# A transformer layer on 8 cores: value projections and expert-0 matmuls placed in three slots inside each layer-norm tile, and a loop exchange in the expert's first matmul

## The reference, cut to what matters

```python
def reference(x, w_in, b_in, w_out, b_out, router_w, w1, b1, w2, b2):
    xn = layernorm(x)                                   # per token, 1024 features
    # attention: att is summed over the key axis of its softmax only, so the
    # output of each head is v itself, times 1
    v = (xn @ w_in.T + b_in)[value part of each head]
    attn = v @ w_out.T + b_out
    # mixture of 8 experts, all of them computed, the best two weighted
    logits = xn @ router_w.T
    top2 values, indices -> softmax of the two -> weights
    h1 = gelu(einsum('bth,efh->btef', xn, w1) + b1)      # 4096 per expert
    y  = einsum('btef,ehf->bteh', h1, w2) + b2
    return x + attn + sum over the two experts of weight * y
```

## Time and profile before

| | us |
|---|---|
| median of 3 runs (4149.61 to 4161.2) | 4151.06 |
| the profiled execution's own time | 4155.26 |
| its span on the slowest core (core 3) | 4153.7 |
| spans of the 8 cores | 4136.3 to 4153.7 |
| mean granted TensorE clock, core 3 | 0.962 |
| PE busy | 3786.6 (91%) |

### The profile page before, as it was taken

One profiled execution on the slowest core, in us unless ns is written; L12 is line 12 of the kernel. 1 busy time (PEld: TensorE's weight loads), 2 busy tenths in 40 slices (PEclk: granted clock), 3 DMA queues, 4 the chain that ended last, 5 costly groups with the idle time before them and its releaser, 6 DMA issues.

```text
span 4153.7 us, 42034 instructions; the slowest of 8 cores (4136.3 to 4153.7 us)
## 1 busy us (share of the span) xinstructions
PE 3786.6 (91%) x17200; PEld 1688.6 (41%) x17200; DVE 372.6 (9%) x626; ACT 627.0 (15%) x610; POOL 667.0 (16%) x1073
## 2 busy tenths in 40 slices
PE   2466799999999999999999999999999999999994
PEld 1122244444444444444444444444444444444442
DVE  3331200000001010000001100000001010000001
ACT  0122102021120203020211202021110203020210
POOL 1001011111111111111111121111111111211110
PEclk9678899999999999999999999999999999999997
DMA  4324245555554555455556455555554555555554
GB/s 74 55 51 69 33 67 76 71 77 76 71 76 72 76 72 82 66 76 72 76 76 112 92 75 73 71 76 71 76 76 72 75 72 76 76 73 71 76 71 106
DMA packets 255706, 307.08 MB, mean 74 GB/s; under 512 B 51687, under 2 KB 182759, under 8 KB 255520
## 3 DMA queue, kind: packets, MB, share of 16 engines
q0 software_dynamic: 248608, 279.23, 48.2%
q1 hardware_dynamic: 6912, 25.17, 1.8%
HBM read 574.89 MB, written 8.39 MB: 140 GB/s over the span
## 4 chain that ended last, share of the span: by engine, by line
PE 88%; DVE 6%; DMA 3%; issue 2%; ACT 1%; DVEq 0%; SPq 0%; POOL 0%; ACTq 0%; POOLq 0%
PE P L339 43%; PE P L419 41%; DVE scr L433 3%; DMA wvw<-wvf 2%; PE P L188 1%; PE P L369 1%; DMA x_rot<-x 1%; PE P L247 1%; ACT vg L350 1%; DVE xnF L253 0%; DMA b1c_sb<-b1c 0%; DVE scr L239 0%; DVEq L46 0%; ACT L232 0%; DVE x_rot L463 0%
## 5 line engine op out<-in xcount | busy, mean ns | idle before, releaser
L419 PE MATMUL P<-wvw,vg 128*128 128x512 bf16 x8192 | 1815.6, 383 | 66.6 <-DVE scr L433 50.9
L339 PE MATMUL P<-xnF,wvw 128*128 128x512 bf16 x8192 | 1783.5, 381 | 6.6 <-DVE scr L433 6.6
L419 PEld LDWEIGHTS P<-wvw,vg 128*128 128x128 bf16 x8192 | 803.2, 99 | 1076.5 <-issue 146.2
L339 PEld LDWEIGHTS P<-xnF,wvw 128*128 128x128 bf16 x8192 | 803.0, 98 | 985.7 <-issue 30.5
L350 ACT ACTIVATE vg<-P,b1c_sb 128x1024 bf16<-128x1024 f32 x512 | 570.7, 1115 | 2850.0 <-PE P L339 2849.9
L396 POOL DMA_DIRECT2D wvw<-w2r x512 | 360.1, 706 | 1586.1 <-PE P L419 1512.0
L322 POOL DMA_DIRECT2D wvw<-w1r x512 | 271.3, 533 | 1555.6 <-PE P L339 1555.6
L433 DVE SCALAR_TENSOR_TENSOR scr<-P,wmap_sb,scr 128x512 f32<-128x512 f32 x256 | 192.1, 750 | 3251.6 <-PE P L419 3227.5
L188 PE MATMUL P<-xnF,wvw 128*128 128x512 bf16 x256 | 88.1, 513 | 46.8 <-DMA wvw<-wvf 46.8
L247 PE MATMUL P<-scr 128*128 128x128 f32 x128 | 26.6, 377 | 99.2 <-DVE scr L239 80.9
L178 POOL DMA_DIRECT2D wvw<-wvf x32 | 28.2, 886 | 276.2 <-PE P L188 276.1
(11 more groups left out here) (40 smaller groups left out, 194.8 us busy)
## 6 DMA issues: line engine op xcount, KB each, us to landing
wvw<-w1r POOLq DMA_DIRECT2D x512, 256.0 KB, 4.3
wvw<-w2r POOLq DMA_DIRECT2D x512, 256.0 KB, 4.4
x_rot<-x SPq DMA_DIRECT2D x32, 512.0 KB, 4.6
wvw<-wvf POOLq DMA_DIRECT2D x32, 256.0 KB, 5.3
out<-x_rot SPq DMA_DIRECT2D x16, 512.0 KB, 3.4
wo_sb<-wo POOLq DMA_DIRECT2D x8, 256.0 KB, 10.8
b1c_sb<-b1c POOLq DMA_DIRECT2D x1, 128.0 KB, 13.8
scr<-iden POOLq DMA_DIRECT2D x1, 64.0 KB, 5.6
```

The costliest lines, as they stand in the source:

```text
L339: pair=pair: t.matmul(pair[:, j * 512:(j + 1) * 512], w1sl[:, sl * 1024 + fc * 128: sl * 1024 + fc * 128 + 128], xnF[:, fc * T + half * 10 ...
L419: t.matmul(W2B[tl], vg[:, f1c * 1024 + tl * 128: f1c * 1024 + (tl + 1) * 128], w2sl[:, sl * 1024 + (f1c % 2) * 512: sl * 1024 + (f1c % 2) ...
```

## The change

There are two parts. The body of `emit_vp_unit` is the body of the loop over `vc` in `emit_vproj`, word for word, and is left out of the diff below.

1. `emit_vproj` is split into `emit_vp_unit(ts, vc)`, one unit each with the same body. `emit_A` calls a function `pump()` at three places: behind the emission of L239 (so on PE ahead of the transposes L247), behind L253 (on PE ahead of the logits) and behind L290 (on PE ahead of the transpose of the weights). Each `pump()` takes the first entry of a list `fills` and emits it, or does nothing where the list is empty. The 8 units of a block enter the list after every fourth tile; the 16 first-matmul groups of expert 0 enter it after tile 7, behind the units of block 1. What is left after tile 15 is emitted in a row.
2. In `emit_h1_group` the two inner loops are exchanged: all 8 matmuls of the first 512 tokens, then the 8 of the second, in place of both for each weight block. This holds for all 512 calls of the inner body, 8192 matmuls.

```diff
-    def emit_vproj(ts):
-        for vc in range(NFC):
...
+    def emit_vp_unit(ts, vc):
...
-    def emit_A(tt):
+    def emit_A(tt, pump):
@@ behind tensor_scalar L239
+        pump()
         p.wait("tensor", "dcst", n_cst)
         p.wait("tensor", "dve", tok_xnt[tt])
@@ end of emit_A
-        if DO_B and tt % 4 == 3:
-            emit_vproj(tt // 4)
@@ emit_h1_group
-            for fc in range(NFC):
-                for j in range(2):
+            for j in range(2):
+                for fc in range(NFC):
                     tok = p.do("tensor",
...
@@ main part
-    for tt in range(8):
-        emit_A(tt)
-    for tt in range(8, NTT):
-        if DO_C:
-            emit_h1_group(0, 0, 2 * (tt - 8))
-            emit_h1_group(0, 0, 2 * (tt - 8) + 1)
-        emit_A(tt)
+    fills = []
+    def pump():
+        if fills:
+            fills.pop(0)()
+    for tt in range(NTT):
+        emit_A(tt, pump)
+        if DO_B and tt % 4 == 3:
+            ts = tt // 4
+            fills += [(lambda ts=ts, vc=vc: emit_vp_unit(ts, vc))
+                      for vc in range(NFC)]
+        if DO_C and tt == 7:
+            fills += [(lambda g=g: emit_h1_group(0, 0, g))
+                      for g in range(NF1C // 2)]
+    while fills:
+        fills.pop(0)()
```

More of the change, by code:

```diff
@@ new lines, in emit_vp_unit @@
+    def emit_vp_unit(ts, vc):
+        idx = 8 * ts + vc
+        pair = SP[idx % 2]
+        sl = vc % 2
+        prev = (ts, vc - 2) if vc >= 2 else ((ts - 1, 6 + vc) if ts >= 1 else None)
+        if prev is not None:
+            p.wait("gpsimd", "pe", tok_vpmm[prev])
+        nqv[sl] += 1
+        p.do("gpsimd", lambda g, vc=vc, sl=sl: g.dma_start(
+            wvf_sl[:, sl * 1024:(sl + 1) * 1024].rearrange(
+                "p (c n) -> p c n", c=NFC),
+            d_wvf[vc].rearrange("c p n -> p c n")), inc=DQ[sl], inc_by=16)
+        wait_pair(idx % 2)
+        p.wait("tensor", DQ[sl], 16 * nqv[sl])
+        p.wait("tensor", "dve", tok_xnFev[4 * ts + 3])
+        vps = pair[:, 0:512]
+        for fc in range(NFC):
+            tok = p.do("tensor", lambda t, fc=fc, sl=sl, ts=ts, vps=vps:
+                       t.matmul(
+                vps,
+                wvf_sl[:, sl * 1024 + fc * 128: sl * 1024 + (fc + 1) * 128],
+                xnF[:, fc * T + ts * 512: fc * T + (ts + 1) * 512],
+                start=(fc == 0), stop=(fc == NFC - 1)),
+                inc=("pe" if fc == NFC - 1 else None))
+        tok_vpmm[(ts, vc)] = tok
+        p.wait("scalar", "pe", tok)
+        tok_vev[idx] = p.do("scalar", lambda s, vc=vc, ts=ts, vps=vps:
+                            s.activation(
+            optF[:, vc * T + ts * 512: vc * T + (ts + 1) * 512],
+            vps, AF.Identity, bias=bvc_sb[:, vc:vc + 1]), inc="act")
+        set_pair(idx % 2, "act", tok_vev[idx])
```

## The result

Over ten runs of each, the ratio of the changed kernel to the kernel before is 0.9747, 95% interval [0.9728, 0.9765]: 4054.6 us (median) against 4154.9. The forecast was 4050, a ratio of 0.976 to the 4151.1 known then.

A forecast was written before the change was run, and what follows sets the result against it. Bound before the output projection: each tile's DVE/ACT/PE chain, taking turns with groups. That stretch falls from 413.7 to 122.0 + 122.0 + 69 = 313 us, a gain of 100.7 against the median 4151.1: 4050, range 4026 to 4082.

The forecast's parts named there:

- What bounds the first 487 us: Ahead of the output projection, a tile's chain alternates between DVE, ACT and PE; groups take turns with it, 27.81 us a period.
- Tiles 4 to 10, 122.0: Value units in slots: five tiles at 16.8 us, tile 7 at 15.5, tile 10 at 22.5; sum 122.0 us.
- Tiles 11 to 15, 5 x 24.4 = 122.0: A group in each slot: 24.4 us for a tile and three groups, against 27.8 with two; five tiles 122.0.
- rival 3: Clock stays at 1.2 GHz through the filled tiles, a group takes 13.65 us in place of 6.9: 4167; chance 0.03.
- lower bound of 22.5: Tiles 11 to 15: 22.5 us for a tile and three groups if PE has no wait at all.
- 16 units in a row, 69: Value units of blocks 2 and 3, without slots, wait for transfers: 8.6 us a pair, 69 us, bounds 62 and 76.
- Part 2, 0 us: Loop exchange in the expert's first matmul: changing weights and 8 matmuls in a row to one bank cost 0 us.
- Rival 1: Tiles 11 to 15: a switch of tables costs twice the 1.38 us seen, 13.5 us more, 4064; chance 0.05.
- Rival 2: In tiles with fills, each unit or group adds its whole length to the tile: 4136 to 4140; chance 0.03.
- The sum: End of tile 3 to output projection: 413.7 us before, 122.0 + 122.0 + 69 = 313 after, gain 100.7.

The follow-up runs named there:

- the complement: The changed kernel with the two inner loops of the expert's first matmul back in their old order: ratio 0.9765 to the kernel before.

## Why the prediction was right, step by step

- *What bounds the first 487 us.* Right. The chain of one tile, taking turns with the fills, is what the change breaks up. The kernel without groups in the second slot shows it for groups at the high clock, the one with overlapped tiles for the tiles themselves.
- *Tiles 4 to 10, 122.0.* Measured 121.5 on core 0 (67.4 + 32.6 + 21.4). Tiles 4 to 6 took 17.2 to 17.4, nearly the low-clock value of 17.5, and tiles 8 and 9 16.3; the 16.8 was a fair mean of two sizes and not one size. Tile 7 is 15.5 as said. Tile 10 was 1.1 quicker on core 0 and took 17.2 to 19.8 on the other seven, against 22.5: the 2.3 that the sum gave its group for the low clock came only in part or not at all (7.3 from 185.61 to 192.92, not 9.2). On the mean of the eight cores the term is 118.6.
- *Tiles 11 to 15, 5 x 24.4 = 122.0.* Measured 122.8: four periods of 24.2 and one of 26.0, the one with a group partly at the low clock; 122.6 on the mean of the cores. The clock, rival 3, did show itself, as 1.8 us and not as 117. The lower bound of 22.5 with no wait at all was no bound: with the tiles overlapped the same work takes 21.9.
- *16 units in a row, 69.* The largest error in the sum on core 0: 63.8 (mean of the cores 63.4). A pair turned over in (372.05 - 315.84) / 7 = 8.03 us and not 8.6; the mean of blocks 0 and 3 took in block 3's 9.35, which did not come back. The cause named, the buffers' turn, is right (four buffers take away 25 to 28 us).
- *Part 2, 0 us.* Right, by itself and as the complement.
- *Rival 1, a switch of tables at twice the price.* Not so: the load begins at 222.80 and Ln at 224.09. The drain that the Trainium skill adds (ScalarE: Activation LUTs, What ACT_TABLE_LOAD costs, 1.38 us more) is in none of these rows: from the Exp's end at 224.68 to the Gelu load at 224.88 is 0.20 us, and the Gelu begins at 226.18.
- *Rival 2.* Not so: a tile with two groups beside the chain takes 18.4 to 18.5 at the high clock and up to 21.6 otherwise, and 27.8 with the groups ahead of it.
- *The sum.* 313.0 forecast, 308.1 on core 0 and 304.5 on the mean of the cores. The start of the output projection fell by 100.4 on the mean, where 100.7 was forecast. That closeness is in part luck, as two errors cancel. The 413.7 us before are those of core 3, the longest; the mean of the eight is 405.0, which is 8.7 less. And the 313 is 8.5 longer than the 304.5, mostly by tile 10 and the row of units. From the slowest core before to the slowest after the start fell by 107.5 (487.1 to 379.6), the executions by 103.8, and the medians of ten by 100.3. The terms as listed reach 26 below 4050, so the range ought to have begun at 4024 and not at 4026; the measured 4054.6 is far from either.

## What to carry to other kernels

When two engines take turns in a chain, find the places in the chain where the busy engine waits, write down how long each wait is, and put work of about that length there; what exceeds a wait is added to the period, and what fits was free here, but for the clock. The order in which fills are used up matters as well: here those that need transfers were left to the end in a row, and the transfers' turn of 8 us per two buffers then became the bound, until more buffers took it away. Where two kinds of fills share PSUM buffers, the hand-over between them has to be in the sum.

## What the runs showed of the hardware that I had not expected

The granted clock fell inside stretches in which PE was busy over 80%. In tile 12 of the changed kernel, with waits of 1.5 and 0.5 and the transposes between the groups, the second group took 8.75 us in place of 7.07, and the clock of the tile is 0.93:

```profile
217.12:243.14 26.02, 23.79 (x112) 10.89 (x114) 8.72 (x21) 12.51 (x13) 3.59 (x6) 0.93 0.45 80
```

Its timeline shows the low level by loads 0.43 us apart, then 0.21:

```profile
227.91 0.15 PEld L339 LDWEIGHTS P<-xnF,wvw 128*128 128x128 bf16 x1 [0.16 <-issue]
228.34 0.15 PEld L339 LDWEIGHTS P<-xnF,wvw 128*128 128x128 bf16 x1 [0.28 <-issue]
...
231.28 4.41 PEld L339 LDWEIGHTS P<-xnF,wvw 128*128 128x128 bf16 x21 [0.23 <-issue]
```

This came in 7 tiles of 40 in the changed kernel and in 28 of 40 with one group less a tile. With the tiles overlapped, where PE has no wait in tiles 12 to 15, it came in none of them. Why it takes one tile and not the next with the same waits is open.

And with four value buffers the 12 transfers of the row (the first four units are loaded before it) were issued from 316.7 on, and the last unit began at 347.4: one in 2.6 us, where with two buffers one came in 4.0. A single such transfer took 6.4 to 7.0 us to land and not 4.7, so the time to land of one transfer says little of how many can be had in a stretch.
